# Selective scan on one core: the three bf16 parts of B and C made by ScalarE copies and TensorE differences, with the order of the front moved

## The reference, cut to what matters

```python
x, res = jnp.split(inputs @ W_in, 2, axis=-1)          # 256 inner channels each
x = jax.nn.silu(_depthwise_conv_same(x, K_conv, b_conv))
delta, Bm, Cm = jnp.split(inputs @ W_x, [64, 80], axis=-1)   # 64 + 16 + 16 columns
delta = jax.nn.softplus(delta @ W_dt + b_dt)
h = exp(delta * A) * h + (delta * x) * Bm              # step by step over 512 positions
y = einsum('bdn,bn->bd', h, Cm)                        # summed over 16 states
out = ((y + x * D) * silu(res)) @ W_out + b_out
```

## Time and profile before

| what | value |
|---|---|
| three runs | 1678.16, 1682.97, 1689.12 us, median 1682.97 us |
| the profiled execution | 1677.74 us |
| its span, first to last instruction | 1675.6 us, so 2.1 us lie outside |
| mean granted clock of TensorE | 0.922 of full speed |
| busy over the whole span | PE 1433.5, DVE 1171.5, ACT 521.5, POOL 528.3 us |
| scan stage in the span | about 752 to 1311 us |

### The profile page before, as it was taken

One profiled execution on the slowest core, in us unless ns is written; L12 is line 12 of the kernel. 1 busy time (PEld: TensorE's weight loads), 2 busy tenths in 40 slices (PEclk: granted clock), 3 DMA queues, 4 the chain that ended last, 5 costly groups with the idle time before them and its releaser, 6 DMA issues.

```text
span 1675.6 us, 21605 instructions
## 1 busy us (share of the span) xinstructions
PE 1433.5 (86%) x7414; PEld 1056.8 (63%) x7414; DVE 1171.5 (70%) x2649; ACT 521.5 (31%) x1011; POOL 528.3 (32%) x448
## 2 busy tenths in 40 slices
PE   3996877795999999985878878878887599999998
PEld 2893545695899999972333333333333389999996
DVE  3666763575676677642798999999999656777753
ACT  2203444200122222213545455355454022222221
POOL 1130000000000000001788888888899100000000
PEclk9997997797999999986889989999998799999998
DMA  4000000001433333201232323332322233333330
GB/s 134 2 1 1 1 1 1 1 1 55 148 102 102 102 102 102 102 1 33 84 90 79 97 68 94 93 79 84 101 84 86 80 124 108 108 109 108 108 108 13
DMA packets 74154, 121.30 MB, mean 72 GB/s; under 512 B 9591, under 2 KB 18750, under 8 KB 73918
## 3 DMA queue, kind: packets, MB, share of 16 engines
q1 hardware_dynamic: 74046, 119.93, 22.9%
HBM read 116.75 MB, written 3.15 MB: 72 GB/s over the span
## 4 chain that ended last, share of the span: by engine, by line
PE 68%; DVE 17%; issue 8%; POOL 4%; ACT 2%; DMA 1%; DVEq 0%; POOLq 0%; ACTq 0%
PE bank L1083 21%; PE bank L1086 7%; PE bank L1201 7%; PE bank L940 5%; PE bank L1145 3%; DVE xe L1567 2%; PE bank L976 2%; DVE both L1559 2%; PE bank L1043 2%; DVE hs L1567 2%; PE bank L1028 2%; POOL both L578 2%; PE bank L1095 2%; PE bank L1025 2%; PE bank L985 1%
## 5 line engine op out<-in xcount | busy, mean ns | idle before, releaser
L1083 PE MATMUL bank<-wqkv_sb,xe 128*128 128x192 f32 x2048 | 369.4, 333 | 10.0 <-DVE xe L1503 9.9
L1083 PEld LDWEIGHTS bank<-wqkv_sb,xe 128*128 128x128 f32 x2048 | 339.1, 194 | 21.4 <-DVE xe L1503 14.9
L1201 PE MATMUL bank<-both,ident 128*128 128x512 f32 x512 | 267.6, 651 | 17.8 <-DVE both L1559 16.8
L546 POOL TENSOR_TENSOR rstd<-ve,half_neg 128x4 f32<-128x4 f32 x32 | 37.5, 1173 | 748.4 <-DVE ve L1254 748.4
L824 ACT ACTIVATE bank<-dt,A 128x512 f32<-128x512 f32 x256 | 172.7, 685 | 167.8 <-DVE xe L1567 93.3
L1201 PEld LDWEIGHTS bank<-both,ident 128*128 128x128 f32 x512 | 104.8, 211 | 151.9 <-issue 108.1
L578 POOL TENSOR_TENSOR both<-du,prob 128x512 f32<-128x512 f32 x128 | 161.0, 1269 | 34.8 <-DVE xe L1567 20.1
L578 POOL TENSOR_TENSOR both<-du,prT 128x512 f32<-128x512 f32 x128 | 160.6, 1269 | 15.3 <-DVE hs L1567 10.7
L1567 DVE TENSOR_TENSOR_SCAN hs<-bank,both 128x512 f32<-128x512 f32 x128 | 153.3, 1208 | 0.0
L1567 DVE TENSOR_TENSOR_SCAN xe<-bank,both 128x512 f32<-128x512 f32 x128 | 152.5, 1208 | 0.0
L940 PEld LDWEIGHTS bank<-exp_sb,xe 128*128 128x128 f32 x1024 | 138.5, 197 | 5.0
(11 more groups left out here) (272 smaller groups left out, 2061.2 us busy)
## 6 DMA issues: line engine op xcount, KB each, us to landing
dt<-w_rows SPq DMA_DIRECT2D x128, 256.0 KB, 4.1
du<-w_rows SPq DMA_DIRECT2D x128, 256.0 KB, 5.0
prob<-bc_dram SPq DMA_DIRECT2D x64, 256.0 KB, 3.3
prT<-bc_dram SPq DMA_DIRECT2D x64, 256.0 KB, 3.3
at<-bc_dram SPq DMA_DIRECT2D x20, 256.0 KB, 3.3
qk_sb<-bc_dram SPq DMA_DIRECT2D x20, 256.0 KB, 3.3
xs<-in_x_dram SPq DMA_DIRECT2D x8, 256.0 KB, 3.8
out_dram<-xs SPq DMA_DIRECT2D x8, 256.0 KB, 2.4
```

Source lines behind the costliest of these rows:

```text
L546: pool.tensor_tensor(rstd[:], ve[:], half_neg[:, 0:NT], ALU.pow).then_inc(ln_rstd, 1)
L1083: m = pe.matmul(bank[4 + j // 2][:, (j % 2) * 3 * HD:(j % 2 + 1) * 3 * HD], x_e, wqkv_sb[:, e, :], start=(e == 0 and j % 2 == 0), stop=(e ...
L1201: pe.matmul(bank[4 + k % NH][:], ident[:], hc[k % HRING], start=False, stop=(SUM_RANK[k] == sums_of(k // UNITS, k % NH))).then_inc(hc_used, 1)
```

## The change

The VectorE step with its six instructions goes, with the matmuls (1138) and the transposes (1159) around it. ScalarE now reads the 32 rows of B and C out of bank 7 once more, as bf16: the first part. TensorE forms in bank 7, on 32 partitions, the fp32 rows minus what the parts so far hold (an fp32 identity matmul and a bf16 matmul with `less`, which is minus one on its diagonals); ScalarE copies that as the second part, and once more for the third. The slots of all later front steps move by one or two, the output projection from slot 6 to 7, its residual add from 8 to 9, and the DMA of the rows from slot 2 to 4.

```diff
-FRONT7 = {"xT": -8, "rows": -6, "conv0": -4, "dlt": 0, "bcT": 2, "conv1": 8, "z0": 12, "z1": 16, "res0": 20, "res1": 22}
-OUT7 = 6
+FRONT7 = {"xT": -6, "conv0": -4, "dlt": 1, "conv1": 9, "z0": 14, "z1": 18, "res0": 22, "res1": 24}
+OUT7 = 7
...
                     act.activation(bc_rows, bank[7][DR:W3, :], ACT.Copy).then_inc(dlt_sb, 1)
-                    yield
-                    act.wait_ge(bank7_ps, seen(IN7["bcT", b]))
-                    act.activation(bcT3[par][:], bank[7][0:W3, 0:L // 2].bitcast(BF16), ACT.Copy).then_inc(bcT_sb, 1)
-                    yield
+                    act.activation(bcT3[par][0:32, :], bank[7][DR:W3, :], ACT.Copy).then_inc(bcT_sb, 1)
+                    yield
+                    for part in (1, 2):
+                        act.wait_ge(part_ps, seen(2 * b + part))
+                        act.activation(bcT3[par][32 * part:32 * (part + 1), :], bank[7][0:32, :], ACT.Copy).then_inc(bcT_sb, 1)
+                        yield
...
-                steps = on_clock(front, (-10, -7, -1, 1, 3, 11, 13, 14, 17, 18, 21, 23))
+                steps = on_clock(front, (-10, -5, -1, 2, 4, 6, 12, 15, 16, 19, 20, 23, 25))
...
-                    into_bank7("rows", b)
-                    for j in range(NT):
-                        m = pe.matmul(bank[7][:, j * 32:(j + 1) * 32], xpad[:, 1 + j * P:1 + (j + 1) * P], wx_sb[:, DR:DR + 32], start=True, stop=True)
-                    m.then_inc(bank7_ps, 1)
-                    yield
...
-                    pe.wait_ge(bc3_made, seen(b + 1))
-                    into_bank7("bcT", b)
-                    rows = bank[7][0:W3, 0:L // 2].bitcast(BF16)
-                    for j in range(NT):
-                        m = pe.transpose(rows[:, j * P:(j + 1) * P], bc3[:, j, :], identb[:])
-                    m.then_inc(bank7_ps, 1)
-                    yield
+                    for part in range(2):
+                        pe.wait_ge(dlt_sb, seen(2 * (b + 1)))
+                        pe.wait_ge(bcT_sb, seen(3 * b + part + 1))
+                        pe.matmul(bank[7][0:32, :], ident[0:32, 0:32], bc_rows, start=True, stop=False)
+                        m = pe.matmul(bank[7][0:32, :], less[0:32 * (part + 1), :], bcT3[par][0:32 * (part + 1), :], start=False, stop=True)
+                        m.then_inc(part_ps, 1)
+                        yield
...
-                steps = on_clock(front, (-8, -6, -4, -2, 0, 2, 8, 10, 12, 16, 20, 22), back, (OUT7,))
+                steps = on_clock(front, (-6, -4, -2, 1, 3, 5, 9, 11, 14, 18, 22, 24), back, (OUT7,))
...
-                    dve.wait_ge(bank7_ps, seen(IN7["rows", b]))
-                    dve.tensor_copy(bc_f[:], bank[7][:, 0:NT * 32].rearrange("p (j e) -> p j e", e=32)).then_inc(rows_read, 1)
-                    dve.wait_ge(rows_read, seen(b + 1))
-                    if b:
-                        dve.wait_ge(bcT_sb, seen(b))
-                    three_parts(bc_f[:], bc_r[:], bc3, 32, bc3_made)
-                    yield
...
-                steps = on_clock(front, (-13, -11, -5, 0, 12, 15, 19, 22, 24), back, (4, 5, 8))
+                steps = on_clock(front, (-13, -11, 1, 14, 17, 21, 24, 26), back, (4, 5, 9))
```

More of the change, by code:

```diff
@@ L317, in macaron @@
         du = [sb(f"du{i}", [P, NH, L]) for i in range(2)]
-        bc_f = sb("bc_f", [P, NT, 32])
-        bc_r = sb("bc_r", [P, NT, 32])
-        bc3 = sb("bc3", [P, NT, W3], BF16)
+        less = sb("less", [64, 32], BF16)
         bcT3 = [sb(f"bcT3{i}", [W3, L], BF16) for i in range(2)]
@@ L384, in macaron @@
             sem(n) for n in ("qkv_sb", "qkT_ps", "qkT_sb", "sc_ps", "nmax_made", "prob_made", "pT_ps", "pT_sb", "at_ps", "at_sb"))
[L386 removed]
+        nmr_made, bank7_ps, part_ps, dlt_sb, g_made, th_made, thr_made, u_made, Du_done, ez_made, ln_made, dt_made, gates_made, \
             bcT_sb, C_ps, dA_made, dB_made, h_made, hc_dve, hc_pool, hc_used, yg_made = (
[L388 to L389 removed]
+                sem(n) for n in ("nmr_made", "bank7_ps", "part_ps", "dlt_sb", "g_made", "th_made", "thr_made", "u_made", "Du_done", "ez_made",
+                                 "ln_made", "dt_made", "gates_made", "bcT_sb", "C_ps",
                                  "dA_made", "dB_made", "h_made", "hc_dve", "hc_pool", "hc_used", "yg_made"))
@@ L480, in scan @@
                 for U in SCAN_CLOCK:
-                    if (U - 2) % UNITS == 0 and 0 <= (U - 2) // UNITS + 1 < NB:
-                        bc_to_dram((U - 2) // UNITS + 1)
+                    if (U - 4) % UNITS == 0 and 0 <= (U - 4) // UNITS + 1 < NB:
+                        bc_to_dram((U - 4) // UNITS + 1)
                     if U % 2 and 0 <= (U + 9) // 2 < NB * NS:
@@ L525, in rest_of_constants @@
                                      allow_small_or_imprecise_dtypes=True))
-                for m in (xpad[:, 0:1], xpad[:, L + 1:L + 4], w3[:], bc3[:]):
+                for m in (xpad[:, 0:1], xpad[:, L + 1:L + 4], w3[:]):
                     chain.link(pool.memset(m, 0.0))
@@ L587, in times_C @@
                     pool.tensor_tensor(hc[k % HRING], hs[k % HRING][:], Cs[n % 2], ALU.mult).then_inc(hc_pool, 1)
-                steps = on_clock(front, (-12, 17, 21))
+                steps = on_clock(front, (-12, 19, 23))
                 for U in SCAN_CLOCK:
@@ L1115, in into_bank7 @@
                         pe.wait_ge(xT_sb, seen(layer * NB + c + 1))
-                    elif last == "rows":
-                        pe.wait_ge(rows_read, seen(c + 1))
-                    elif last == "bcT":
-                        pe.wait_ge(bcT_sb, seen(c + 1))
                     elif last == "dlt":
-                        pe.wait_ge(dlt_sb, seen(2 * (c + 1)))
+                        pe.wait_ge(bcT_sb, seen(3 * (c + 1)))
                     elif last == "out":
@@ L1185, in spread_C @@
                     if s % NS == 0:
[L1186 removed]
+                        pe.wait_ge(bcT_sb, seen(3 * (s // NS + 1)))
                     if d >= 2:
@@ L1235, in _ @@
             link(dve.tensor_copy(identb[:], ident[:]))
+            link(dve.tensor_scalar(less[:], pick32[0:64, :], -1.0, None, ALU.mult))
             link(dve.tensor_copy(pick[:], pick32[:].unsqueeze(2).to_broadcast([W3, 32, P])))
```

4 lines of the change are left out of this document (removed).

## The result

The changed kernel takes 1686.97 us, median of 13 runs (1684.79 to 1693.38), against 1681.76 (1677.88 to 1689.12, 13 runs) for the kernel before on the same chip: ratio 1.0039, 95% interval 1.0024 to 1.0053. It is 5 us slower, within what the prediction called no change; forecast was 1658, and the range ended at 1673. The profiled execution took 1687.6 us with a span of 1685.5, 9.9 more than before.

A forecast was written before the change was run, and what follows sets the result against it. VectorE was taken to set the 65.0 us pass, waiting for others twice. Terms of -27 + 2.4 + 1.5 - 1.5 = -24.6 us gave 1653.1 profiled; with the median 5.2 above the profiled run, 1658 us, range 1642 to 1673.

The forecast's parts named there:

- The clock: TensorE in a pass: idle before the delta, B and C matmul shrinks from 3.19 to under 1 us, moving to slots 23 to 26.
- rival four: Differences through projection at 1.2 GHz after short gaps; with 9 us added wait, pass 4.5 us longer, 1708 us; chance 0.06.
- The sum: All terms together: -27 + 2.4 + 1.5 - 1.5 = -24.6 us, profiled execution 1677.74 to 1653.1, median forecast 1658.
- the prediction's own sign of being wrong: TensorE, slots 5 to 14: a granted clock under 0.9 there would show the forecast wrong.
- The waits of a pass: VectorE's waits in a steady pass: 3.9 us against 3.5 before, so 0.4 more a pass, 2.4 us in six.
- the walk: Slot-by-slot timing of a changed pass: new waits 1.3, 0.7, 0.7, 0.4 and 0.8 us; unit 8 and second u waits go.
- The step of the three parts: VectorE's six instructions making B and C parts, sequences 2 to 7: removal saves 4.5 us each, 27 us in all.
- u of the first half: VectorE's u at slot 1, after the later transpose: 0.3 us spare or some 1.4 wait at low clock, taken as 0.8.
- ScalarE at no cost: ScalarE's added copies in slots 2, 4 and 6: busy time grows 1.2 us a pass, off the path, cover 1.1 us.
- TensorE's 1.1 us a difference: Two differences in slots 3 and 5, one fp32 and one bf16 matmul each: 1.1 us a difference, ends 0.7 and 2.4.
- The two ends: Fronts of sequences 0 and 1 and the last pass: net -1.6 to +0.6, taken as -1.5 us; last pass nothing.

The follow-up runs named there:

- e3: Changed kernel with both matmuls of each difference over the full array (128 input rows for the fp32 one, 128 output columns): 1671.07 us, ratio 0.9943.
- e11: Changed kernel with the fp32 matmul of each difference taking 128 input rows, still writing 32 partitions: 1669.54 us, ratio 0.9924.
- e7: Changed kernel, 32-partition differences kept, with the coming spread of C issued three times more in each of slots 4 and 5: 1684.62 us, ratio 1.0021.
- e12: Changed kernel, 32-partition differences kept, with the spread of C repeated in slots 4 and 5 and in slots 24 and 25: 1668.09 us, ratio 0.9914.
- e8: Changed kernel with its differences widened on the output side only, 128 columns of weights, input rows as before: 1691.58 us, ratio 1.0069.
- e2: Changed kernel without TensorE's two differences; ScalarE copies the same rows three times, order unchanged: 1671.35 us, ratio 0.9942.
- e9: Changed kernel with full-array differences as in e3, plus the spread of C repeated three times in slot 24 and six in slot 25: 1659.44 us, ratio 0.9873.
- e1: Kernel before, old order, with VectorE's step cut to the copy and one cast, second and third parts left unmade: 1675.01 us, ratio 0.9965.
- e13: Kernel before with its old parts in the changed kernel's slots, plus the spread of C repeated in slots 24 and 25: 1674.44 us, ratio 0.9965.
- e4: Kernel before, three parts still made on VectorE, with the changed kernel's slots: 1675.94 us, ratio 0.9970.

## Why the prediction was wrong

**The failed step** is "The clock", with the reason given against rival four: "after 944 TensorE has no gaps, and now it comes to full clock in that stretch by itself". The sum gives the clock no term. TensorE was at full clock there from 940.44 on, and lost it at 947.5, in the middle of the stretch, in every pass; over slots 5 to 14 of the pass shown (946.05 to 968.93) the mean granted clock is 0.85, and under 0.9 there was the prediction's own sign of being wrong. What the runs show in place of "by itself": in this stretch the clock stayed full when the differences had 128 rows (e3, e11) or when the gap between them was filled (e7, e12), and it fell when they had 32 rows (the changed kernel, e8) or were not there at all (e2). So the small matmuls did no more for the clock than the empty slots did, and what they added was their own time at the low level, ahead of a wait. The prediction priced the differences by the time they take and not by whether they keep the clock up. Rival four had the place, and the short gaps as the cause, but not the part of the 32 rows, and less than half of its price came: its low stretch was to last from the differences to the projection, 9 us a pass; it lasted from the second difference through half of the sums and cost 3.46 or 1.77 us. A second fall, ahead of the product of unit 30, cost up to 3.7 us in four passes. With both held off (e9) a pass takes 61.4 us, where the forecast had about 61.

**The waits of a pass.** Forecast 3.9 us, measured 8.5 of idle time. What is over is the two waits for sums at the low clock, of the product of unit 8 and of the product of unit 30. The second one was half seen: "the idle time moves to the waits for the gates, in slots 23 to 26"; what is late behind those gaps was given to u of the first half at most, and the walk stopped short of the next spread of C. With both falls out of the way (e9) the walk is right in four of its five places and in its total: 1.55 before the residual add (forecast 1.3), 1.04 behind the second four sums (0.7), dt and gate 0.25 and 0.24 (0.7 and 0.4), 3.84 in all with 0.76 at the end (3.9), and a pass of 61.4 (61). That the total agrees to a tenth is in part luck: the forecast 0.8 at the end was for u of the first half, which does not wait; the 0.76 stand ahead of the product of unit 30, which the walk has without a wait.

**The step of the three parts.** Right in itself, and 1.0 us of it came back elsewhere. Here are its six instructions in the five passes of the kernel before, and below them the line that moved with the order (busy us, mean ns):

```profile
L1279 DVE CAST bc<-bc_f 128x128 bf16<-128x128 f32 x5 | 5.8, 1151 | 0.2
L1280 DVE TENSOR_TENSOR bc_r<-bc_f,bc 128x128 f32<-128x128 f32 x5 | 5.3, 1062 | 0.2
L1281 DVE CAST bc<-bc_r 128x128 bf16<-128x128 f32 x5 | 4.9, 986 | 0.2
L1282 DVE TENSOR_TENSOR bc_r<-bc_r,bc 128x128 f32<-128x128 f32 x5 | 4.4, 870 | 0.2
...
L1516 DVE COPY bc_f<-bank 128x128 f32<-128x128 f32 x5 | 1.4, 278 | 0.0
L1513 DVE SCALAR_TENSOR_TENSOR nmr<-mv,rstd 128x4 f32<-128x4 f32 x5 | 1.3, 267 | 0.0
L1283 DVE CAST bc<-bc_r 128x128 bf16<-128x128 f32 x5 | 1.1, 227 | 0.2
```

The six sum to 22.9 us, 4.6 a pass; 4.5 was forecast. But VectorE's busy time fell by only 3.6 a pass. The small instruction for nmr takes longer:

```profile
L1505 DVE SCALAR_TENSOR_TENSOR nmr<-mv,rstd 128x4 f32<-128x4 f32 x5 | 4.1, 816 | 0.0
```

It takes 0.82 us instead of 0.27, which is 0.55 of the 1.0; slightly longer scans and products (means of 1211 ns after 1208, and 664 after 660) are another 0.2, and the rest was not taken apart. GpSimd works beside it in both kernels; what moved is where in a GpSimd instruction it falls. In one middle pass of the kernel before it starts at 976.10, when GpSimd's product of 975.09 to 976.35 is nearly over, and ends at 976.36; in the changed kernel it starts at 983.10, early in a product that starts at 982.70 and takes 1.25 us, and ends at 983.99. The prediction had priced the neighbourhood of GpSimd for what was removed and not for what was moved. The Trainium skill, SBUF — State Buffer, section Who interferes with whom, has the rule that an instruction with two SBUF inputs contends with one of GpSimd that reads SBUF. These rows agree: same instruction, same size, and both times it ends when GpSimd's does.

**Small terms.** ScalarE at no cost held: no decay was late behind a copy in a middle pass, and a copy of the parts took 0.57 to 0.59. TensorE's 1.1 us a difference was 1.25 at full clock (944.05 to 945.30) and 2.34 at the low one (947.52 to 949.86), inside the bounds of 0.7 to 2.4. The two ends were forecast at -1.5: the first skip matmul comes at 816.82 instead of 812.93, of which 2.9 us had already passed before the stage began, so +1.0 in the front of sequence 0.

**The sum again.** Forecast -24.6; measured +9.9 in the profiled executions, 2.9 of it before the stage, so 31.6 us apart. In the five middle passes 24: forecast -4.1 each, measured +0.76, of which idle time explains 4.0 (+4.4, forecast +0.4) and busy time 0.9 (-3.6, forecast -4.5). In the front of sequence 0 2.5. The remaining 5 lie in the first pass and the last ones, and I did not take them apart.

## What to carry to other kernels

Work taken off VectorE does not come off a pass one for one, even where VectorE is the busiest: 3.0 us gave 0.7 where the low clock moved into a stretch that VectorE waits for (e1), 4.3 gave 3.1 with the clock out of the way (e9 against e13). Before taking work off, look up where in the pass the granted clock falls now, and whether TensorE is waited for there or has slack. The place of the fall is movable: some 7 us at the low clock cost VectorE nothing ahead of the filled gaps in e9, and as many cost 3.5 us ahead of a wait in the changed kernel. Of matmuls that are added, look at the input rows as well as at the time: if they use 32 rows, feed all 128 with zeros in the weights (e11), and where a gap cannot be closed, repeat a matmul whose result is overwritten anyway, but only behind a wait that is long over.

## What the runs showed of the hardware that was not expected

An fp32 matmul over 512 columns takes the same time with 32 rows or with 128: two pieces 1.04 and 1.02 us. The Trainium skill, TensorE: Matmul & The Clock Gate, section Why this matters for your kernels, says so of a single matmul with 32 rows, and the rows agree. What follows differs: behind the small one the clock fell to 1.2 GHz in slots 6 to 8 of every pass, behind the full one, at the same idle time, it did not (the times: 1686.97 against 1671.07 us; 1691.58 for 32 rows and 128 columns, 1669.54 for 128 rows and 32 columns). With no difference at all and 2.16 and 0.40 us of idle time (e2) it fell there too. How rows and idle time weigh against each other was not measured.

A fall that is held off in one place can turn up in another (e7), and the mean granted clock does not rank the kernels: it is 0.96 in the five passes of e13 with 64.5 us a pass, and 0.94 in those of e9 with 61.4. e2 and e7 have passes of 64.9 and 64.8 us, as have e4 in its last two and the kernel before in three of five, from different waits. Why these agree is open.
